# Second attention of a two-layer transformer kernel: the projection back as split products, with ScalarE, VectorE and GpSimd sharing its copies anew

## The reference, cut to what matters

```python
x = seq * rsqrt(mean(seq * seq, -1) + eps) * g_norm      # seq: the conditioned batch
q, k, v = split(x @ W_qkv)                               # 16 heads of 64
q, k = rotary(q), rotary(k)                              # 2 segments of 128 positions
k, v = concat((pm[0], k)), concat((pm[1], v))            # 16 extra positions
attn = softmax(where(mask, q @ k.T / 8, -1e30))
out = (attn @ v).reshape(..., 1024) @ W_out              # the projection back
x = x + out
```

## Time and profile before

| | us |
|---|---|
| median of 3 runs | 2487.05 (2486.1 to 2489.55) |
| the profiled execution, its own time | 2490.11 |
| its span, first to last instruction | 2488.4 |
| TensorE busy | 2356.3 |
| VectorE, ScalarE, GpSimd busy | 1849.6, 1253.7, 1019.8 |
| mean granted TensorE clock | 0.977 of full |

### The profile page before, as it was taken

How to read it: one execution, slowest core, us unless ns; L and a number is a source line. 1 busy time by engine, 2 the same in 40 slices (tenths; PEclk the granted TensorE clock), 3 DMA queues, 4 the chain that set the end, 5 groups by cost and what they waited for, 6 DMA issues and landing times.

```text
span 2488.4 us, 54483 instructions
## 1 busy us (share of the span) xinstructions
PE 2356.3 (95%) x18880; PEld 2094.2 (84%) x18880; DVE 1849.6 (74%) x5116; ACT 1253.7 (50%) x3771; POOL 1019.8 (41%) x1074
## 2 busy tenths in 40 slices
PE   4899999999987799999999999899999999999999
PEld 3687878878866688888888887799999999999999
DVE  6777777777777766666666665568877888888876
ACT  2656665666654355455455455334325555555522
POOL 4645546455443544544544545123322222222063
PEclk7999999999998899999999999899999999999999
DMA  4311211212120222122122122121116677777443
GB/s 120 109 43 46 58 46 47 47 46 59 35 86 9 65 53 55 42 50 55 41 52 54 42 53 64 47 69 39 40 41 219 227 238 230 241 228 235 154 119 124
DMA packets 153079, 225.71 MB, mean 91 GB/s; under 512 B 54294, under 2 KB 123174, under 8 KB 142054
## 3 DMA queue, kind: packets, MB, share of 16 engines
q1 hardware_dynamic: 143942, 203.56, 28.1%
q0 software_dynamic: 8864, 18.66, 2.9%
HBM read 159.32 MB, written 27.16 MB: 75 GB/s over the span
## 4 chain that ended last, share of the span: by engine, by line
PE 71%; DVE 10%; issue 8%; ACT 7%; POOL 2%; DMA 1%; SPq 0%; POOLq 0%; ACTq 0%; DVEq 0%
PE bank L55 55%; PE bank L136 7%; PE bank L1250 2%; PE bank L339 2%; ACT P L1446 2%; PE bank L366 1%; PE bank L1291 1%; ACT Ph L621 1%; DVE xe L884 1%; ACT PTh L633 1%; ACT L1494 1%; POOL P L1723 1%; DVE Ph L770 1%; DVE xe L887 1%; DVE sgs L908 1%
## 5 line engine op out<-in xcount | busy, mean ns | idle before, releaser
L1446 ACT ACTIVATE P<-P,mx 128x144 f32<-128x144 f32 x512 | 206.4, 404 | 347.5 <-DVE mx L1556 347.5
L55 PE MATMUL bank<-xD_hi,w1e_lo 128*128 128x256 f32 x880 | 251.8, 286 | 0.0
L2549 POOL DMA_INDIRECT xE<-d_y,ixs x78 | 111.7, 1433 | 339.6 <-PE bank L136 312.0
L55 PE MATMUL bank<-w2e_hi,hrD_hi 128*128 128x256 f32 x880 | 249.0, 283 | 0.0
L55 PE MATMUL bank<-w2e_lo,hrD_hi 128*128 128x256 f32 x880 | 248.9, 283 | 0.0
L55 PE MATMUL bank<-w2e_hi,hrD_lo 128*128 128x256 f32 x880 | 248.9, 283 | 0.0
L1076 POOL TENSOR_TENSOR xe<-xe 128x704 f32<-128x704 f32 (+3 forms) x64 | 88.3, 1380 | 388.3 <-DVE xe L889 388.0
L55 PE MATMUL bank<-xD_lo,w1e_hi 128*128 128x256 f32 x880 | 246.6, 280 | 0.0
L55 PE MATMUL bank<-xD_hi,w1e_hi 128*128 128x256 f32 x880 | 246.3, 280 | 0.0
L2158 ACT ACTIVATE hD<-bank,b1E 128x256 f32<-128x256 f32 x312 | 126.9, 473 | 197.3 <-PE bank L55 183.2
L1723 POOL TENSOR_TENSOR P<-P,rs 128x512 f32<-128x512 f32 x128 | 133.1, 1040 | 182.2 <-DVE rs L1565 177.4
(11 more groups left out here) (318 smaller groups left out, 7813.6 us busy)
## 6 DMA issues: line engine op xcount, KB each, us to landing
w1raw<-in_ew SPq DMA_DIRECT2D x39, 1024.0 KB, 6.0
w2raw<-in_ew SPq DMA_DIRECT2D x39, 1024.0 KB, 4.9
K<-Kn SPq DMA_DIRECT2D x256, 72.0 KB, 2.1
Q<-Qn SPq DMA_DIRECT2D x256, 64.0 KB, 2.0
d_ys<-oE SPq DMA_DIRECT2D x39, 256.0 KB, 2.4
d_rot<-QK SPq DMA_DIRECT2D x16, 512.0 KB, 2.9
Rs<-d_rot SPq DMA_DIRECT2D x64, 128.0 KB, 4.2
b2E<-in_eb SPq DMA_DIRECT2D x39, 128.0 KB, 3.4
```

Source lines behind the costliest of these rows:

```text
L55: inst = e.matmul(out, l, r, start=k == 0, stop=k == len(pairs) - 1)
L1446: inst = e.activation(P1[t % 2][:, n, :], P1[t % 2][:, n, :], ACT.Exp, bias=mx1[t % 2][:, 2 * g + sg:2 * g + sg + 1], scale=-1.0, accum_ou ...
L2549: e.indirect_dma_start(out=xE[q % 2][c], out_offset=None, in_=d_y, in_offset=bass.IndirectOffsetOnAxis(ap=ixs[r % 4][:, c:c + 1].bitcast(U ...
```

## The change

`OT1` and `wo1` become pairs of `hi` and `lo`, and the projection back uses `matmuls3`: 24 products where there were 8. ScalarE's `out_copy` now copies both banks to the high parts, one after the other, and comes before the exponentials in steps 0 and 4; the last copy of V moves to the front of step 0. VectorE's `out_copy` is replaced by `out_low`, two subtractions that make the low parts. The subtraction that makes the rest of the normed batch moves from VectorE (after the turned copy of step 5) to GpSimd (behind combinations 5 and 6 of step 5). To make room, Q and K have one buffer each, and stacking a half of batch `b` waits for batch `b - 1`'s scores of that half. The weights arrive in a buffer of V and are split in steps 1, 2, 3 and 5 of batch 0.

```diff
-        Q1, K1, V1 = [tile("Q10", 8, 256)], [tile("K10", 8, 288)], [tile("V10", 2, 1024)]
+        Q1, K1, V1 = tile("Q1", 8, 256), tile("K1", 8, 288), [tile("V10", 2, 1024)]
...
-        OT1, wo1, pmv = tile("OT1", 8, 256), tile("wo1", 8, 256), tile("pmv", 8, 128)
+
+        rawo = V1[1].rearrange("p s (f n) -> p (s f) n", n=256)
+        OT1, wo1, pmv = pair("OT1", 8, 256), pair("wo1", 8, 256), tile("pmv", 8, 128)
...
             for b in range(B):
-                if b >= 2:
-                    e.wait_ge(p_S1, 8 * (b - 1))
                 for half in range(2):
                     e.wait_ge(g_r1, 8 * b + 4 * half + 4)
+                    if b >= 1:
+                        e.wait_ge(p_S1, 8 * (b - 1) + 4 * half + 4)
...
                         e.dma_start(pmv, a["pmv"]).then_inc(l_pm[0], 16)
-                if b == 0:
-                    e.dma_start(wo1, a["wo1"]).then_inc(l_co, 16)
+                        e.dma_start(rawo, a["wo1"]).then_inc(l_co, 16)
...
-                matmuls(e, back_bank(b)[:, d, :], [(wo1[:, f, d * 128:d * 128 + 128], OT1[:, f, :])
-                                                for f in range(8)]).then_inc(p_back, 1)
+                matmuls3(e, back_bank(b)[:, d, :], [
+                    (cut(wo1, lambda x: x[:, f, d * 128:d * 128 + 128]), cut(OT1, lambda x: x[:, f, :]))
+                    for f in range(8)]).then_inc(p_back, 1)
...
-                e.activation(OT1[:, 4 * half:4 * half + 4, 0:128], quarters(4), ACT.Copy).then_inc(c_O1, 1)
+                for sg in range(2):
+                    e.activation(OT1[0][:, 4 * half:4 * half + 4, 128 * sg:128 * sg + 128], quarters(4 + sg), ACT.Copy
+                                 ).then_inc(c_O1, 1)
...
+            def split_back(f):
+
+                e.wait_ge(l_co, 16)
+                e.activation(wo1[0][:, f:f + 2, :], rawo[:, f:f + 2, :], ACT.Copy).then_inc(c_w1, 1)
...
-                    exps(t + 1)
+                    if s == 0:
+                        values_copy(b, 1, 1)
                     if s % 4 == 0:
                         out_copy(t - 1)
+                    exps(t + 1)
...
-                    if s == 0:
-                        values_copy(b, 1, 1)
...
+                    if b == 0 and s in (1, 2, 3, 5):
+                        split_back(2 * (1, 2, 3, 5).index(s))
```

On VectorE and GpSimd:

```diff
-            def out_copy(t):
+            def out_low(t):
                 if not 0 <= t < 8 * B or t % 4 != 3:
                     return
...
-                e.tensor_copy(OT1[:, 4 * half:4 * half + 4, 128:256], quarters(5)).then_inc(v_O1, 1)
+                half = t // 4 % 2
+                for sg in range(2):
+                    at = (slice(None), slice(4 * half, 4 * half + 4), slice(128 * sg, 128 * sg + 128))
+                    e.wait_ge(c_O1, t // 4 * 2 + sg + 1)
+                    inst = e.tensor_tensor(OT1[1][at], quarters(4 + sg), OT1[0][at].bitcast(F32), ALU.subtract)
+                inst.then_inc(v_O1, 1)
...
-            def x_low(b):
-                if not 0 <= b < B:
-                    return
-                e.wait_ge(c_xr, b + 1)
-                e.tensor_tensor(xr[b % 2][1], fa, xr[b % 2][0].bitcast(F32), ALU.subtract).then_inc(v_xrlo, 1)
...
+            def split_back(f):
+                e.wait_ge(c_w1, 7 + f // 2)
+                e.tensor_tensor(wo1[1][:, f:f + 2, :], rawo[:, f:f + 2, :],
+                                wo1[0][:, f:f + 2, :].bitcast(F32), ALU.subtract).then_inc(v_w1, 1)
...
-                    if s == 5:
-                        x_low(entering(b))
...
+            def x_low(b):
+                if not 0 <= b < B:
+                    return
+                e.wait_ge(c_xr, b + 1)
+                e.tensor_tensor(xr[b % 2][1], fa, xr[b % 2][0].bitcast(F32), ALU.subtract).then_inc(g_xrlo, 1)
+                e.wait_ge(g_xrlo, b + 1)
...
                     if s == 5:
                         combine(b + 1, 5)
                         combine(b + 1, 6)
+                        x_low(entering(b))
+                    if b == -3 and s == 7:
+                        x_low(0)
```

More of the change, by code:

```diff
@@ L1169, in program @@
             "S1", "T1", "PV1", "qk1", "V1", "lap", "one", "back"))
-        v_mx1, v_ri1, v_PT1, v_O1, v_t7, v_rn, v_xn, v_xrlo, v_x1r, v_back, v_w1 = (sem(f"v_{n}") for n in (
-            "mx1", "ri1", "PT1", "O1", "t7", "rn", "xn", "xrlo", "x1r", "back", "w1"))
+        v_mx1, v_ri1, v_PT1, v_O1, v_t7, v_rn, v_xn, v_x1r, v_back, v_w1 = (sem(f"v_{n}") for n in (
+            "mx1", "ri1", "PT1", "O1", "t7", "rn", "xn", "x1r", "back", "w1"))
         c_P1, c_PT1, c_V1, c_O1, c_sq, c_rt, c_xr, c_w1 = (sem(f"c_{n}") for n in (
             "P1", "PT1", "V1", "O1", "sq", "rt", "xr", "w1"))
-        g_n1, g_r1, g_const = sem("g_n1"), sem("g_r1"), sem("g_const")
+        g_n1, g_r1, g_const, g_xrlo = sem("g_n1"), sem("g_r1"), sem("g_const"), sem("g_xrlo")
         proj_bank = (0, 1, 1, 0, 0, 1, 0, 1)
@@ L1210, in stack @@
                         at, j, steps = 64 * (i % 2) + 32 * eo, 2 * half, slice(4 * half + i // 2, 4 * half + i // 2 + 3, 2)
-                        for dst, src in ((Q1[b % 2], Qn), (K1[b % 2], Kn)):
+                        for dst, src in ((Q1, Qn), (K1, Kn)):
                             e.dma_start(dst[at:at + 32, steps, :], src[32 * i:32 * i + 32, j:j + 2, eo, :]
@@ L1250, in scores @@
                         inst = e.matmul(bank[g][:, 144 * sg:144 * sg + 144],
-                                        Q1[par][64 * g:64 * g + 64, s, 128 * sg:128 * sg + 128],
-                                        K1[par][64 * g:64 * g + 64, s, 144 * sg:144 * sg + 144], start=True, stop=True)
+                                        Q1[64 * g:64 * g + 64, s, 128 * sg:128 * sg + 128],
+                                        K1[64 * g:64 * g + 64, s, 144 * sg:144 * sg + 144], start=True, stop=True)
                 inst.then_inc(p_S1, 1)
@@ L1477, in values_copy @@
                     e.wait_ge(p_PV1, 8 * (b - 1))
+                elif b:
+                    e.wait_ge(v_w1, 10)
                 e.activation(V1[b % 2][:, sg, 512 * c:512 * c + 512], banks[c][:, :], ACT.Copy).then_inc(c_V1, 1)
@@ L1603, in differences @@
                     e.wait_ge(p_one, b)
-                    e.wait_ge(v_xrlo, b)
+                    e.wait_ge(g_xrlo, b)
                 else:
@@ L1675, in dve_c @@
                         normalize(0)
-                    if b == -3 and s == 7:
-                        x_low(0)
                     invert(t)
@@ L1691, in dve_c @@
                     if s % 4 == 0:
-                        out_copy(t - 1)
+                        out_low(t - 1)
                     if s == 0:
@@ L1836, in program @@
             "h", "x", "f2", "R", "yD", "lg", "marks", "rk", "slot", "tab", "cb", "w2E"))
-        WC = WD = 6
+        WC = WD = 10
         WE = WD + 3
```

15 lines of the change are left out of this document (3 added, 12 removed).

## The result

The kernel after takes **2510.21 us** (median of 4 runs, 2504.71 to 2511.92), the kernel before beside it 2488.18 us: a ratio of 1.0085 with a 95% interval of [1.0074, 1.0097], 21 us slower by the ratio and 22 us by the medians. I had forecast 2503 us, in a range of 2490 to 2520, and slower with a chance of 0.84. The profiled execution took 2510.2 us around a span of 2508.5 us, 20.1 us more than before.

What follows compares the result with a forecast made beforehand. A chain through ScalarE, VectorE and GpSimd was taken as level with TensorE. +1.15 us a batch made +15.0 us over 13, plus +1.2 us once: 2506.3 us profiled, 2503 us as median, range 2490 to 2520 us.

Steps and rivals of the forecast that it cites:

- The half of step 2: Projection back's half ahead of step 3's start: split products move the whole chain 0.51 us earlier per full batch.
- V's copy: Moved to the front of ScalarE's step 0: gains 0 of TensorE's 0.6 us wait, since VectorE paces steps 0 to 2.
- The half of step 3: Projection back's half beside ScalarE's root and VectorE's norm: its 0.51 us saving is waited away at step 4.
- The low half at step 4: VectorE's one copy becomes two subtractions where it has no gap: +0.61 us on the chain per batch.
- The rest on GpSimd: Subtraction in GpSimd's step 5, ahead of step 6's normalisation: +1.38 us, less 0.33 us from a combination no longer slowed.
- ScalarE's doubled copy: Two output copies ahead of the exponentials in steps 0 and 4: delay hidden in ScalarE's waits, cost 0.
- Batch 0: Weight splitting in steps 1 and 2 costs +2.4 us, steps 3 and 5 have room; GpSimd's addition about +1.0 us.
- Batch 14: No field or norm, TensorE alone the bound: two halves and V's wait give -1.6 us.
- The stage's end: Batch 15 and after: four halves save 2.0 us, doubled copy loses 0.5 and 0.9 us in two places: -0.6 us.
- TensorE is the only bound: Rival: GpSimd's rest is done before step 6's turn, batches keep both halves and V's wait; 2466 us, chance 0.10.
- GpSimd's delay is absorbed: Rival: V's earlier copy or VectorE free in step 5 shortens each batch 0.6 to 1.2 us; 2490 us, chance 0.09.
- The waits cost clock: Rival: TensorE's granted clock falls in each full batch, 3.4 us at half costing 1.7 us; 2525 us, chance 0.06.

Runs made afterwards that it cites:

- v_first: Kernel before with only V's last copy moved to the front of ScalarE's step 0; ratio to before 0.9990, batch 46.87 us.
- late_v_last: Kernel after, rest in step 7, add-back before norm, weights split in steps 3 and 5, V's last copy behind exponentials; ratio to before 1.0017.
- half1_plain: Kernel after with step 3's half of the projection back as 8 full-precision products of the high parts; ratio to before 1.0093, batch 48.08 us.
- exps_first: Kernel after with ScalarE's old order, exponentials ahead of output copies and V's copy behind both; ratio to before 1.0326, batch 52.2 us.
- before_add_first: Kernel before with the add-back moved ahead of the norm on VectorE in step 4; ratio to before 0.9999, batch 46.89 us.
- split_late: Kernel after with batch 0's weights split in steps 3 and 5 only, two pieces each; ratio to before 1.0077, batch 0 47.62 us.
- rest_late: Kernel after with the rest's subtraction still on GpSimd but in step 7 instead of 5; ratio to before 1.0025, batch 47.01 us.

## Why the prediction was right, point by point

**The full batch** was forecast at 48.0 us and took 48.07. Term by term:

- *The half of step 2, −0.51*: the products took 3.04 us as worked out, the step shortened by 0.59 us (v_first, 8.08, to after, 7.49), and undoing the half cost 0.63 us. Yet steps 0 to 2 together shortened only by 18.91 − 18.52 = 0.39 us. The 0.20 us between are the low half of step 0, for which the sum had 0. The rotation moved 0.21 us, near the 0.25 forecast, but the gap before the copy of the turned did not take it up: it is 0.40 us in v_first and in the kernel after alike, so the copy moved along with the rotation. In the kernel before, the field ends 13.00 us after step 0 begins, in v_first 13.00, in the kernel after 13.20, and TensorE's fourth projection waits for it in each batch.
- *V's copy, 0*: right by luck of two parts, 0.29 us gained and as much lost (0.27 on the mean of 13). The lost part is a term that the sum did not have, the field's first operation, with two inputs in SBUF, beside a combination of GpSimd. The group by line, in the kernel after and then in the kernel before:

```profile
L1626 DVE TENSOR_TENSOR fa<-fa,X 128x512 f32<-128x512 f32 x13 | 12.7, 973 | 0.0
```

```profile
L1617 DVE TENSOR_TENSOR fa<-fa,X 128x512 f32<-128x512 f32 x13 | 9.2, 705 | 0.0
```

  In the profiled batch GpSimd's addition runs from 1200.85 to 1201.59 and this operation starts at 1201.15. In the kernel before they overlapped by 0.12 us. That V's copy alone brings it is shown by v_first (975 ns) and late_v_last (682 ns). I had treated such slowing on one side only, for GpSimd in step 5.
- *The half of step 3, 0*: right, and shown by half1_plain.
- *The low half at step 4, +0.61*: the rotation moved 0.59 us, and filling VectorE's wait with the add-back took back 0.58.
- *The rest on GpSimd, +1.38 − 0.33 = +1.05*: 1.37 us from start to start, 0.33 us back from the sums, and 1.0 to 1.06 us when it left.
- *ScalarE's doubled copy, 0*: right. But this zero and V's are not independent. The copy's is bought by its place ahead of the exponentials (exps_first) and by V's ahead of it (late_v_last).

Steps 3 to 6 together grew by 24.31 − 22.69 = 1.62 us; forecast was 0.61 + 1.05 = 1.66. So +1.15 us were forecast and +1.22 found: 0.08 us too little gain for the half and 0.20 us too little cost for the low half partly cancel.

**What happens once** was the mis-sized term, forecast at +1.2 us and found at +4.2. By the starts of scores it is +2.6 us up to batch 0, +5.05 in batch 0 (forecast +3.4), −0.96 in batch 14 (forecast −1.6), +1.03 from there to the stage's last scores, and −3.5 us in the third stage. The first and the last can't be laid to the change: batch 0 begins at 845.5 us in the kernel before and at 847.0 in before_add_first, with the same code up to there, and the third stage took 926 to 934 us in four kernels on one chip that differ only ahead of it. Their near cancelling is luck.

*Batch 0.* Its step 4, in the view of stretches: before; before_add_first, whose work in this batch is the same as before's; after; split_late.

```profile
870.62:879.39 8.77, 6.87 (x51) 5.97 (x50) 5.88 (x20) 5.31 (x16) 1.78 (x3) 0.81 0.45 107
872.14:882.34 10.20, 8.30 (x51) 7.39 (x50) 5.88 (x20) 5.32 (x16) 2.62 (x4) 0.67 0.41 98
874.18:884.86 10.68, 7.63 (x51) 6.73 (x50) 6.69 (x20) 7.46 (x19) 1.33 (x2) 0.68 0.36 85
873.54:884.41 10.87, 8.04 (x50) 7.17 (x49) 8.04 (x22) 6.83 (x19) 1.38 (x3) 0.69 0.39 92
```

TensorE's wait in it, before and after, and between them the second piece of the weights' split in the kernel after (step 2's, on VectorE):

```profile
873.28 0.80 PE L1286 MATMUL bank<-PmT,pmv 64*128 64x128 f32 x4 [1.90 <-ACT PmT L1459]
...
871.04 0.69 DVE L1670 TENSOR_TENSOR wo_lo<-V,wo_hi 128x512 fp32r<-128x512 f32 x1 [1.25 <-ACT wo_hi L1519]
...
877.99 0.80 PE L1285 MATMUL bank<-PmT,pmv 64*128 64x128 f32 x4 [3.05 <-ACT PmT L1458]
```

The pieces of steps 1 and 2 cost 1.5 us (split_late) where I had 2.4. I had taken 1.25 us for each from the earlier trace rows; they took 0.68 and 0.69 us, but the second also waited 1.25 us for ScalarE's high part. Behind it the maxima, the exponentials, the root and the copies of the turned came later, so TensorE waited 3.05 us for 1.90. With no piece in steps 1 and 2, split_late has the 1.90 us again, and step 3 at 4.88 us as before. The rest on GpSimd cost 1.3 us (rest_late) for 1.0, and V's earlier copy gave back 0.4 us here (v_first, 43.72 for 44.11). If these parts add up, that leaves 2.6 of the +5.05 us, mostly in step 4, which the forecast did not have. Some 1.4 us of it need not be the change's: before_add_first has before's work and before's wait of 1.90 us, yet its clock stood at half for longer and the step took 10.20 us. What failed in my reasoning is "step 3 has it waiting for the root": that piece waits for ScalarE's high part, which stands behind the root and the copies, so it ran at 878.49, ahead of the norm, which began 1.7 us after the root was done. In split_late TensorE waits 0.94 us for the norm. How much of the last 1.2 us this is stays open.

*Batch 14.* Two halves give 2 × 0.59 us, the low half of step 0 takes 0.20, and V's copy gives nothing here either (v_first, 43.16 us for 43.17): −0.97 us, and −0.96 was found. So the forecast's 0.6 us for V's wait was wrong, and TensorE was not alone the bound there.

*The stage's end.* The forecast of −0.6 us counted four halves, of which two lie behind the last scores, in what is the third stage above. Up to the last scores the doubled copy costs most in the last step. In the view of stretches, before, after and rest_late, with TensorE's wait in each:

```profile
1568.37:1573.38 5.01, 2.68 (x27) 1.80 (x26) 3.35 (x13) 3.77 (x18) 1.33 (x2) 0.96 0.01 3
1590.43:1596.97 6.54, 3.83 (x26) 2.66 (x25) 4.42 (x14) 4.53 (x22) 1.33 (x2) 0.70 0.01 3
1570.77:1577.33 6.56, 3.10 (x26) 2.19 (x25) 4.42 (x14) 4.54 (x22) 1.33 (x2) 0.86 0.01 2
...
1570.23 0.49 PE L1286 MATMUL bank<-PmT,pmv 64*128 64x128 f32 x4 [1.10 <-ACT PmT L1459]
1593.00 0.77 PE L1285 MATMUL bank<-PmT,pmv 64*128 64x128 f32 x4 [1.81 <-ACT PmT L1458]
1573.35 0.49 PE L1285 MATMUL bank<-PmT,pmv 64*128 64x128 f32 x4 [1.81 <-ACT PmT L1458]
```

The step grew by 1.5 us. It is as long at a granted clock of 0.86 as at 0.70, since its turn waits for GpSimd's Pm and that for VectorE, where the doubled low half stands in the queue. From the step's scores to that turn it is 5.29 us for 4.17: 1.12 us for the 0.9 that I had. The turn up to the next scores takes the other 0.4 us, at half clock.

Sum: 2.6 + 5.05 + 15.9 + 0.1 − 3.5 = 20.1 us, the spans' difference. The forecast of 16.2 us had the batches right within 1 us. The 3 us by which what happens once was missed are no more than what the same code varied by between these executions (1.4 us in step 4 of batch 0, 8 us in the third stage), so that the total came as near as it did is in part luck.

**The rivals.** *TensorE is the only bound* is out: it had 11.1 us less to do in the full batches, and they lasted 15.9 us longer. *GpSimd's delay is absorbed* is out: it came off at full price. *The waits cost clock* did not come true where I had put it: the full batches have 1.00, with waits of TensorE's products up to 0.9 us. Outside them the clock stood at half for longer than before, but the same happened in before_add_first without longer waits. And exps_first shows what it costs once a wait of 2.65 us stands in every batch: it fell in ten of 13, for 0.9 us a batch on the mean where I had priced 1.7.

## What to carry to other kernels

When two chains are level, ask of each moved operation what stands right behind it in its new queue: the same 1.29 us cost 1.06 us a batch ahead of a normalisation that TensorE waits for, and nothing two steps later. A saving on the level engine counts only where it lies ahead of the chain's first link (half 0), or where the other engine's work is reordered to use it (half 1 with the add-back first); the reordering without the saving, or the saving without the reordering, gives nothing. And an operation that costs nothing by its place in a queue should be listed with that place, since the price comes back at once when the order is changed.

## What the runs showed of the hardware

VectorE and GpSimd slow each other when both read two operands from SBUF, and both can pay at once: GpSimd's sum of 128x256 took 1.05 us for 0.73 beside VectorE's subtraction, and that subtraction 1.25 us where one of the same size took 0.68 beside an idle GpSimd. VectorE's addition of 128x512 took 0.97 us for 0.68 beside GpSimd's sum. The rotations and the low parts, which read one operand from PSUM, kept their time whatever GpSimd did (675 and 684 ns in the groups of the kernel after, 652 to 692 ns each). The Trainium skill (SBUF — State Buffer, Who interferes with whom) says that a VectorE instruction with at most one input in SBUF, outside VectorE's two-port modes, doesn't contend with GpSimd, and one with two does when GpSimd reads SBUF; these rows agree, and a kernel that moves work from one of the two engines to the other should look for such pairs in both directions.

The length of the wait just before does not by itself tell whether TensorE's clock falls. In the second attention it fell from 2.4 to 1.2 GHz, for some 3 to 7 us, near waits of 1.58, 1.81, 1.90, 2.65 and 3.05 us. But the same waits also passed: 1.58 us in before_add_first (granted clock 1.00 from 1550 to 1560 us), 1.81 us in rest_late (1.00 from 1554 to 1560 us), and 2.65 us in three of 13 batches of exps_first. And the same wait of 1.90 us was followed by about 3.4 us at half clock in the kernel before and by about twice that in before_add_first. It stayed behind waits of 0.88 us, once in each 48 us through 625 us, and behind one of 1.33 us in batch 14. What decides between is not shown here. So no single place shows what a wait costs in clock: compare several executions or kernels in which the same wait stands.
